# A fused two-layer decoder on one core: the top-32 search cut into fifteen pieces of two segments per head, and GpSimd adding two pairs of heads with one instruction

## The chip, the cores and the metric

The kernel runs as one launch on one core of a Trainium2 chip. The metric is the device time of that launch in microseconds (us), as the median over runs. A core has five engines with instruction streams of their own that meet only at semaphores: TensorE (PE), VectorE (DVE), ScalarE (ACT), GpSimd (POOL) and SyncE (SP).

## The reference, cut to what matters

The whole is a decoder of two layers over `x` (1024 tokens x 128 numbers) and a context of 6404 rows x 96. The stage that the change touches is the sparse cross-attention of the second layer:

```python
B, T, DT, G, DV = ...            # here 1, 1024, 128, 6404, 96
H, DH, K_TOP = 4, 32, 32
Q = (x_text @ Wq).reshape(Bb, Tt, H, DH)
K = (x_vision @ Wk).reshape(Bb, Gg, H, DH)
scores = jnp.einsum('bthd,bghd->bhtg', Q, K) / np.sqrt(DH)
topv, topi = jax.lax.top_k(scores, K_TOP)
probs = jax.nn.softmax(topv, axis=-1)
attn = zeros_like(scores).at[bi, hi, ti, topi].set(probs)
attn_mean = attn.mean(axis=1)                       # over the four heads
c_t = jnp.einsum('btg,bgd->btd', attn_mean, x_vision @ Wv)
```

For each token and head the 32 largest of 6404 scores are wanted, their softmax, and the mean of the four heads' sparse weights multiplied with the context.

## The kernel before, in words

`weigh_program` (called by `search_and_weigh`) does this stage. Tokens go in 8 tiles of 128, each with 4 heads, so 32 heads in all. Two streams of work run side by side.

**Search.** For each head, PE computes the scores piece by piece into one of 3 PSUM banks (`SEARCH_BANKS`), by two bf16 matmuls a piece (`score_unit`, L1461 and L1463). There are 13 pieces, twelve of 512 columns and one of 260 (`PIECES`). DVE takes the eight largest of each segment of a piece with `dve.max` (L1665, MAX8 in the profile): a 512 piece has three segments of 170 or 171 columns, the 260 piece two of 130, so a head has 38 segments (`N_SEG`) and 304 candidates in `kept`. Then `pick` takes the 32 largest of these candidates in eight steps, which are woven into the search of the next head: one reduction (L1640), four MAX8 (L1648) and three replacements (L1646), all over the whole row of candidates. If a segment's eighth value is above the 32nd found, the head is flagged and `search_general` and `weigh_again` do the work anew in another way.

**Weighing.** A step `n` is one piece of `PIECES` for one tile, so there are 104 steps. For each of its 4 heads PE computes the scores again into one of 3 other banks, ACT takes the exponential into `e` (L1847; a ring of 4 steps), and values under the 32nd are set to zero: heads 0 and 1, and head 2 in every other step, on DVE (L1695); the rest by a mask that ACT makes (L1825, L1826) and POOL multiplies (L1718). In the last tile DVE does all four, and adds two of them. POOL then adds the four heads to `mean` (L1722, L1726, L1727), PE transposes it (L1739), ACT copies the result (L1804), and PE multiplies with the context (L1752). At the first step of each tile the limits of the four heads are made by a short chain between DVE and ACT (L1678, L1853, L1682, L1856, L1686 to L1688, L1859).

**Order.** Each engine's order is written out: loops over `G` (a step) and `sub` (a head), and in each such slot one piece of the search and one head of the weighing. The weighing of a tile runs `LAG` = 15 steps behind the search, so the search is alone for 15 steps at the start, and the weighing is alone for the last 15.

## Time and profile before

| what | value |
|---|---|
| median of 3 runs | 1744.25 us (1743.5 to 1744.35) |
| profiled execution, its time | 1739.54 us |
| its span, first to last instruction | 1737.8 us |
| mean granted TensorE clock | 0.912 of full |
| the stage's first matmul, last DVE search instruction, last POOL addition (starts) | 642.5 us, 1211.3 us, 1275.25 us |

Times in the rows count from the start of the span. In a row of a timeline the number in square brackets is how long the engine was idle before it, and what released it. "Busy" is the union of the instructions' durations; consecutive instructions on DVE overlap in their durations, so what an instruction costs in a dense row is the distance between starts.

### The profile page before, as it was taken

To read this page: it belongs to the slowest core of one execution; us is meant where nothing else is said; L and a number is where in the kernel's file an instruction comes from. 1 tells how busy PE (TensorE), PEld (TensorE's weight loads), DVE (VectorE), ACT (ScalarE), POOL (GpSimd) and SP (SyncE) were. 2 spreads that over 40 slices of the span, in tenths; PEclk is the share of its full clock that TensorE was granted. 3 is DMA by queue.
4 is the path that set the end of the run, shared out by engine and by line. 5 is a ranking of instruction groups with operands and counts; after the bars stand their busy time and mean duration, and the time that the engine had idled before them with its cause. 6 is when DMAs were issued, how large, how long until landed. Compare 5 with 4: busy or idle time off the path is not lost. (4 is left out here: it accounts for less than half of the span.)

```text
span 1737.8 us, 19863 instructions
## 1 busy us (share of the span) xinstructions
PE 1420.6 (82%) x6581; PEld 752.1 (43%) x6637; DVE 1288.2 (74%) x3067; ACT 930.5 (54%) x1452; POOL 697.0 (40%) x529
## 2 busy tenths in 40 slices
PE   5777899899986747889898888988859339999798
PEld 2233344345544421355454554545547223333365
DVE  4998677855427539999999999999857666777433
ACT  4665212556521310788888888888831225666321
POOL 0664312012000000698898988989930030000012
PEclk9899899999987867999999999999888758999999
DMA  6000110000009320000000000000011030000000
GB/s 145 1 1 0 39 61 29 0 1 0 0 19 198 68 64 1 1 1 1 1 1 1 1 1 1 1 1 1 1 27 71 22 80 1 1 1 1 1 1 12
DMA packets 30968, 37.36 MB, mean 21 GB/s; under 512 B 13889, under 2 KB 24096, under 8 KB 29732
## 3 DMA queue, kind: packets, MB, share of 16 engines
q1 hardware_dynamic: 29312, 24.19, 5.1%
q10 hardware_dynamic: 1544, 11.79, 3.3%
q8 instruction: 56, 0.92, 0.2%
q14 instruction: 56, 0.46, 0.1%
HBM read 29.73 MB, written 6.24 MB: 21 GB/s over the span
## 5 line engine op out<-in xcount | busy, mean ns | idle before, releaser
L1461 PE MATMUL psum<-film_ka,film_context_qa 97*128 97x512 bf16 (+1 forms) x832 | 326.0, 393 | 86.8 <-DVE search_and_weigh_e L1695 36.5
L1665 DVE MAX8 search_and_weigh_kept<-psum 128x8 f32<-128x171 f32 (+2 forms) x1216 | 330.1, 324 | 0.2
L1463 PE MATMUL psum<-film_kb,film_context_qb 128*128 128x512 bf16 (+1 forms) x777 | 302.0, 390 | 0.0
L1847 ACT ACTIVATE search_and_weigh_e<-psum,search_and_weigh_bias 128x512 f32<-128x512 f32 (+1 forms) x416 | 267.5, 665 | 58.0 <-PE psum L1463 54.7
L1695 DVE SCALAR_TENSOR_TENSOR search_and_weigh_e<-psum,film_context_top,search_and_weigh_e 128x512 f32<-128x512 f32 (+1 forms) x283 | 200.0, 714 | 15.5 <-ACT search_and_weigh_e L1847 14.0
L1718 POOL TENSOR_TENSOR search_and_weigh_e<-search_and_weigh_e,search_and_weigh_keep 128x512 f32<-128x512 f32 (+1 forms) x133 | 150.6, 1132 | 108.6 <-ACT search_and_weigh_keep L1826 105.3
L1461 PEld LDWEIGHTS psum<-film_ka,film_context_qa 97*128 97x128 bf16 x832 | 86.3, 104 | 229.8 <-DVE search_and_weigh_e L1695 95.5
L1722 POOL TENSOR_TENSOR search_and_weigh_mean<-search_and_weigh_e 128x512 f32<-128x512 f32 (+1 forms) x104 | 133.4, 1283 | 11.5 <-DVE search_and_weigh_e L1695 4.4
L1752 PEld LDWEIGHTS psum<-ctx_rows,search_and_weigh_mean_T 128*128 128x128 f32 (+1 forms) x816 | 124.1, 195 | 31.3 <-issue 5.2
L2959 POOL TENSOR_TENSOR residual<-residual,top_expert_kept 128x1024 f32<-128x1024 f32 x7 | 16.5, 2355 | 292.2 <-DVE top_expert_kept L2916 292.2
L1727 POOL TENSOR_TENSOR search_and_weigh_mean<-search_and_weigh_mean,search_and_weigh_e 128x512 f32<-128x512 f32 (+1 forms) x104 | 127.9, 1230 | 8.2
L2722 DVE TENSOR_REDUCE gqa_attend_low<-psum 128x1 f32<-128x128 f32 (+7 forms) x128 | 94.0, 754 | 43.2 <-PE psum L2641 40.7
L1752 PE MATMUL psum<-ctx_rows,search_and_weigh_mean_T 128*128 128x96 f32 (+1 forms) x816 | 121.0, 271 | 1.0
L1726 POOL TENSOR_TENSOR search_and_weigh_e<-search_and_weigh_e 128x512 f32<-128x512 f32 (+1 forms) x91 | 111.8, 1229 | 7.1
L2759 ACT ACTIVATE gqa_attend_prob<-psum 128x512 f32<-128x512 f32 x192 | 84.9, 486 | 49.6 <-PE psum L2654 48.9
L1039 ACT ACTIVATE cross_attention_prob<-psum 128x1024 f32<-128x1024 f32 (+1 forms) x51 | 51.8, 1019 | 97.1 <-PE psum L998 96.4
L340 POOL TENSOR_TENSOR mamba_drive<-mamba_relu,mamba_b_all 128x1024 f32<-128x1024 f32 x32 | 77.2, 2414 | 64.7 <-ACT mamba_b_all L465 33.6
L985 PE MATMUL psum<-cross_attention_prob,ctx_rows 128*97 128x512 f32 (+1 forms) x204 | 98.2, 604 | 4.6 <-ACT cross_attention_prob L1039 4.6
L1825 ACT ACTIVATE search_and_weigh_keep<-search_and_weigh_e,search_and_weigh_below 128x512 bf16<-128x512 f32 (+1 forms) x133 | 93.5, 703 | 12.7 <-POOL search_and_weigh_mean L1727 12.2
L998 PE MATMUL psum<-oss_attention_qc_shifted,ctx_T 97*128 97x512 f32 (+1 forms) x204 | 99.3, 610 | 0.8 <-ACT oss_attention_qc_shifted L1030 0.8
L1463 PEld LDWEIGHTS psum<-film_kb,film_context_qb 128*128 128x128 bf16 x832 | 84.5, 102 | 33.4 <-issue 6.0
L1739 PE MATMUL psum<-ident,search_and_weigh_mean 128*128 128x128 f32 (+1 forms) x408 | 81.3, 281 | 11.7 <-ACT search_and_weigh_mean_T L1804 9.3
(544 smaller groups left out, 2660.1 us busy)
## 6 DMA issues: line engine op xcount, KB each, us to landing
film_kb<-film_k_rows ACTq DMA_DIRECT2D x4, 1601.0 KB
film_ka<-film_k_rows ACTq DMA_DIRECT2D x3, 1601.0 KB
ctx_T<-in_ctx_T SPq DMA_DIRECT2D x1, 2401.5 KB
gqa_experts_w<-in_L_ffn_W SPq DMA_DIRECT2D x1, 2048.0 KB
film_convolve_back<-in_dft_back SPq DMA_DIRECT2D x1, 1728.0 KB, 11.9
film_k_rows<-cross_attention_film_hi SPq DMA_DIRECT2D x6, 256.0 KB, 2.0
film_k_rows<-cross_attention_film_mid SPq DMA_DIRECT2D x6, 256.0 KB, 2.0
film_k_rows<-cross_attention_film_low SPq DMA_DIRECT2D x6, 256.0 KB, 2.0
```

The lines of the kernel that those rows point to most:

```text
L985: last = pe.matmul(ps[0:CA, 6 + n, :], ctx[0:rows, k, :], prob[0:rows, k % 3, n * HALF:(n + 1) * HALF], start=k == 0, stop=k == KT - 1)
L998: last = pe.matmul(ps[0:rows, 2 * (k % 2) + n, :], ctx_T[:, k * P:k * P + rows], qc_shifted[:, n * HALF:(n + 1) * HALF], start=True, stop= ...
L1461: pe.matmul(out, a["qa"][0:ROWS, h, rows], a["ka"][0:ROWS, h, c + b:c + b + cols], start=True, stop=False)
L1463: last = pe.matmul(out, a["qb"][:, h, rows], a["kb"][:, h, c + b:c + b + cols], start=False, stop=True)
L1665: last = dve.max(kept[:, h % 2, first + s, :], bank[:, lo:hi])
L1695: dve.scalar_tensor_tensor(out=w, in0=weigh_bank(n, h), scalar=a["top"][:, NH * i + h, TOP - 1:TOP], in1=w, op0=ALU.is_ge, op1=ALU.mult).t ...
L1718: link(pool.tensor_tensor(w[h], w[h], keep[:, k % KEEPS, 0:width], ALU.mult))
L1722: link(pool.tensor_tensor(out, w[0], w[1], ALU.add))
L1726: link(pool.tensor_tensor(w[2], w[2], w[3], ALU.add))
L1727: pool.tensor_tensor(out, out, w[2], ALU.add).then_inc(mean_ready, 1)
L1752: last = pe.matmul(ps[:, 7, 0:DC], mean_T[0:r, n % 2, b:b + P], ctx[0:r, (c + b) // P, 0:DC], start=c + b == 0, stop=c + b + r == S2)
L1847: act.activation(e[:, n % RING, sub, 0:PIECES[u][1]], ps[:, SEARCH_BANKS + q % WEIGH_BANKS, 0:PIECES[u][1]], ACT.Exp, bias=bias[:, i % 2, ...
```

## The change

The search no longer uses the weighing's pieces. A head's 6404 columns are cut into 30 nearly equal segments of 213 or 214 columns, two to a piece, so 15 pieces of 426 or 427 columns in place of 13. As there are 13 slots of the weighing per head and 15 pieces, `searched_at` deals them: in slots 6 and 12 of each 13, two pieces stand, in the others one. On POOL, two adds of two heads each (`w[0]+w[1]` to `mean`, `w[2]+w[3]` in place) become one in-place instruction over both pairs, and the last add takes `w[0]+w[2]`. In the last tile POOL's adds stay as they were. The core of the diff:

```diff
-def segments(width):
-    n = -(-width // 171)
-    edges = [round(k * width / n) for k in range(n + 1)]
-    return list(zip(edges[:-1], edges[1:]))
-N_SEG = sum(len(segments(w)) for _, w in PIECES)
+SEARCHES, PER_PIECE = 15, 2
+N_SEG = SEARCHES * PER_PIECE
+SEARCH_EDGES = [round(k * S2 / N_SEG) for k in range(N_SEG + 1)]
+
+def search_columns(u):
+    edges = SEARCH_EDGES[PER_PIECE * u:PER_PIECE * (u + 1) + 1]
+    return edges[0], edges[-1] - edges[0], [(lo - edges[0], hi - edges[0]) for lo, hi in zip(edges[:-1], edges[1:])]
...
+    def searched_at(G, sub):
+        k = NH * G + sub
+        return range(k * SEARCHES // NCH, (k + 1) * SEARCHES // NCH)
...
         for G in range(STEPS + LAG + 1):
             for sub in range(NH):
-                r = NH * G + sub
-                head, after = r // NCH - 1, r % NCH
+                for r in searched_at(G, sub):
+                    head, after = r // SEARCHES - 1, r % SEARCHES
...
             pool.wait_ge(w_ready, masks_done(n + 1))
-            if n >= MEANS:
-                pool.wait_ge(mT_psum, n - MEANS + 1)
-            link(pool.tensor_tensor(out, w[0], w[1], ALU.add))
             if last_tile(n):
+                if n >= MEANS:
+                    pool.wait_ge(mT_psum, n - MEANS + 1)
+                link(pool.tensor_tensor(out, w[0], w[1], ALU.add))
                 pool.wait_ge(summed_ready, n + 1 - (NT - 1) * NCH)
+                pool.tensor_tensor(out, out, w[2], ALU.add).then_inc(mean_ready, 1)
             else:
-                link(pool.tensor_tensor(w[2], w[2], w[3], ALU.add))
-            pool.tensor_tensor(out, out, w[2], ALU.add).then_inc(mean_ready, 1)
+                pairs = e[:, n % RING, :, 0:width].rearrange("p (a b) k -> p a b k", b=2)
+                link(pool.tensor_tensor(pairs[:, :, 0, :], pairs[:, :, 0, :], pairs[:, :, 1, :], ALU.add))
+                if n >= MEANS:
+                    pool.wait_ge(mT_psum, n - MEANS + 1)
+                pool.tensor_tensor(out, w[0], w[2], ALU.add).then_inc(mean_ready, 1)
...
-                search(NH * G + sub + SEARCH_LEAD)
+                for r in searched_at(G, sub):
+                    search(r + SEARCH_LEAD)
```

On POOL, the first two steps of the weighing read before:

```order
L1718 TENSOR_TENSOR search_and_weigh_e<-search_and_weigh_e,search_and_weigh_keep 128x512
L1722 TENSOR_TENSOR search_and_weigh_mean<-search_and_weigh_e 128x512
L1726 TENSOR_TENSOR search_and_weigh_e<-search_and_weigh_e 128x512
L1727 TENSOR_TENSOR search_and_weigh_mean<-search_and_weigh_mean,search_and_weigh_e 128x512
L1718 TENSOR_TENSOR search_and_weigh_e<-search_and_weigh_e,search_and_weigh_keep 128x512 x2
```

The same place after the change (L1725 is the former L1718, L1735 the new add of two pairs, L1738 the last add):

```order
L1725 TENSOR_TENSOR search_and_weigh_e<-search_and_weigh_e,search_and_weigh_keep 128x512
L1735 TENSOR_TENSOR search_and_weigh_e<-search_and_weigh_e 128x2x512
L1738 TENSOR_TENSOR search_and_weigh_mean<-search_and_weigh_e 128x512
L1725 TENSOR_TENSOR search_and_weigh_e<-search_and_weigh_e,search_and_weigh_keep 128x512 x2
L1735 TENSOR_TENSOR search_and_weigh_e<-search_and_weigh_e 128x2x512
```

Three additions a step have become two, and the first stands where an instruction of half its width stood.

On DVE, just behind the limits of a tile (the small operations on `bias` and `least`), before:

```order
L1688 TENSOR_TENSOR search_and_weigh_least<-film_context_top,search_and_weigh_bias 128x4
L1695 SCALAR_TENSOR_TENSOR search_and_weigh_e<-psum,film_context_top,search_and_weigh_e 128x260
L1665 MAX search_and_weigh_kept<-psum 128x8 x6
L1695 SCALAR_TENSOR_TENSOR search_and_weigh_e<-psum,film_context_top,search_and_weigh_e 128x512
L1665 MAX search_and_weigh_kept<-psum 128x8 x3
L1695 SCALAR_TENSOR_TENSOR search_and_weigh_e<-psum,film_context_top,search_and_weigh_e 128x512
L1665 MAX search_and_weigh_kept<-psum 128x8 x3
L1695 SCALAR_TENSOR_TENSOR search_and_weigh_e<-psum,film_context_top,search_and_weigh_e 128x512
L1665 MAX search_and_weigh_kept<-psum 128x8 x3
L1640 TENSOR_REDUCE film_context_eighth<-search_and_weigh_kept 128x1
```

After the change (L1695, L1702, L1672 and L1648 are the former L1688, L1695, L1665 and L1640):

```order
L1695 TENSOR_TENSOR search_and_weigh_least<-film_context_top,search_and_weigh_bias 128x4
L1702 SCALAR_TENSOR_TENSOR search_and_weigh_e<-psum,film_context_top,search_and_weigh_e 128x260
L1672 MAX search_and_weigh_kept<-psum 128x8 x4
L1702 SCALAR_TENSOR_TENSOR search_and_weigh_e<-psum,film_context_top,search_and_weigh_e 128x512
L1672 MAX search_and_weigh_kept<-psum 128x8 x2
L1702 SCALAR_TENSOR_TENSOR search_and_weigh_e<-psum,film_context_top,search_and_weigh_e 128x512
L1672 MAX search_and_weigh_kept<-psum 128x8 x2
L1702 SCALAR_TENSOR_TENSOR search_and_weigh_e<-psum,film_context_top,search_and_weigh_e 128x512
L1672 MAX search_and_weigh_kept<-psum 128x8 x5
L1648 TENSOR_REDUCE film_context_eighth<-search_and_weigh_kept 128x1
```

A slot has two segments where it had three, and the doubled slot at the end of a head has four, with a fifth that begins the next head.

On PE, at a doubled slot after the change (L1464 and L1466 are the former L1461 and L1463; 426 or 427 columns are a piece of the search, 512 one of the weighing; L1763 and L1750 the former L1752 and L1739):

```order
L1466 MATMUL psum<-film_kb,film_context_qb 128x512
L1750 MATMUL psum<-ident,search_and_weigh_mean 128x128 x2
L1464 MATMUL psum<-film_ka,film_context_qa 128x426
L1466 MATMUL psum<-film_kb,film_context_qb 128x426
L1464 MATMUL psum<-film_ka,film_context_qa 128x427
L1466 MATMUL psum<-film_kb,film_context_qb 128x427
L1464 MATMUL psum<-film_ka,film_context_qa 128x512
```

Before, one pair of L1461 and L1463 for the search stood there, ahead of the pair for the weighing; now the weighing's matmul stands behind two pairs.

## Rows read from the trace of the kernel before

**Rows 1.** Busy time of each engine over the span, from the page.

```profile
PE 1420.6 (82%) x6581; PEld 752.1 (43%) x6637; DVE 1288.2 (74%) x3067; ACT 930.5 (54%) x1452; POOL 697.0 (40%) x529
```

**Rows 2.** Windows of the stage; columns: PE, PEld, DVE, ACT, POOL busy, PEclk, DMA.

```profile
646.60:703.90 57.30, 42.86 (x120) 10.95 (x123) 57.06 (x232) 3.65 (x6) 0.00 (x0) 0.74 0.00 1
...
784.87:859.93 75.06, 66.57 (x357) 37.72 (x363) 72.71 (x235) 64.33 (x113) 68.91 (x58) 0.98 0.00 1
...
935.01:1010.10 75.09, 66.62 (x357) 37.80 (x363) 72.78 (x235) 64.41 (x113) 68.87 (x59) 0.98 0.00 1
...
1233.00:1276.00 43.00, 38.19 (x243) 27.62 (x247) 40.43 (x61) 36.31 (x62) 37.60 (x27) 1.00 0.01 1
```

**Rows 3.** Timeline of POOL: first weighing, two full steps, a tile's boundary.

```profile
709.82 1.16 POOL L1718 TENSOR_TENSOR search_and_weigh_e<-search_and_weigh_e,search_and_weigh_keep 128x512 f32<-128x512 f32 x1 [89.38 <-ACT search_and_weigh_keep L1826]
...
922.85 2.38 POOL L1718 TENSOR_TENSOR search_and_weigh_e<-search_and_weigh_e,search_and_weigh_keep 128x512 f32<-128x512 f32 x2
925.31 1.26 POOL L1722 TENSOR_TENSOR search_and_weigh_mean<-search_and_weigh_e 128x512 f32<-128x512 f32 x1
926.66 1.27 POOL L1726 TENSOR_TENSOR search_and_weigh_e<-search_and_weigh_e 128x512 f32<-128x512 f32 x1
928.01 1.26 POOL L1727 TENSOR_TENSOR search_and_weigh_mean<-search_and_weigh_mean,search_and_weigh_e 128x512 f32<-128x512 f32 x1
...
929.98 0.73 POOL L1722 TENSOR_TENSOR search_and_weigh_mean<-search_and_weigh_e 128x260 f32<-128x260 f32 x1
...
935.01 1.16 POOL L1718 TENSOR_TENSOR search_and_weigh_e<-search_and_weigh_e,search_and_weigh_keep 128x512 f32<-128x512 f32 x1 [2.67 <-ACT search_and_weigh_keep L1826]
...
1233.00 1.29 POOL L1722 TENSOR_TENSOR search_and_weigh_mean<-search_and_weigh_e 128x512 f32<-128x512 f32 x1
```

**Rows 4.** Waits in one period, 935.01 to 1010.1: waiter, releaser, total us, times, longest.

```profile
PEld psum L1461 <- DVE search_and_weigh_e L1695: 12.3, 19, 1.9
ACT search_and_weigh_e L1847 <- PE psum L1463: 7.0, 9, 1.4
POOL search_and_weigh_e L1718 <- ACT search_and_weigh_keep L1826: 5.4, 2, 2.7
...
ACT search_and_weigh_keep L1825 <- POOL search_and_weigh_mean L1727: 1.7, 3, 1.1
DVE search_and_weigh_e L1695 <- ACT search_and_weigh_e L1847: 1.6, 4, 0.6
```

**Rows 5.** Timeline of DVE where the search is alone.

```profile
656.55 0.20 DVE L1640 TENSOR_REDUCE film_context_eighth<-search_and_weigh_kept 128x1 f32<-128x38 f32 x1
...
662.17 2.98 DVE L1665 MAX8 search_and_weigh_kept<-psum 128x8 f32<-128x171 f32 x12
...
693.21 0.20 DVE L1640 TENSOR_REDUCE film_context_eighth<-search_and_weigh_kept 128x1 f32<-128x38 f32 x1
```

**Rows 6.** Durations by tile `kept`: min/median/max ns, first and last start, forms.

```profile
L1665 DVE MAX8 search_and_weigh_kept<-psum x1216: 273/325/345, 646.6 to 1211.3; 128x8 f32<-128x171 f32 x110, 128x8 f32<-128x170 f32 x55, 128x8 f32<-128x130 f32 x9
L1648 DVE MAX8 film_context_top<-search_and_weigh_kept x128: 450/457/478, 657.2 to 1216.7; 128x8 f32<-128x304 f32 x128
```

**Rows 7.** Groups of POOL over the whole span: count, busy us, mean ns, idle.

```profile
L340 POOL TENSOR_TENSOR mamba_drive<-mamba_relu,mamba_b_all 128x1024 f32<-128x1024 f32 x32 | 77.2, 2414 | 64.7 <-ACT mamba_b_all L465 33.6 <-DVE mamba_relu L280 28.6 <-issue 2.1
L646 POOL TENSOR_TENSOR ss_attention_s4d_i_decay<-cross_attention_s4d_ar,ross_attention_s4d_index 128x1024 f32<-128x1024 f32 x16 | 31.2, 1960 | 131.1 <-DVE ss_attention_s4d_i_angle L612 127.5 <-DVE ross_attention_s4d_turns L544 3.6
L2959 POOL TENSOR_TENSOR residual<-residual,top_expert_kept 128x1024 f32<-128x1024 f32 x7 | 16.5, 2355 | 292.2 <-DVE top_expert_kept L2916 292.2
```

**Rows 8.** Timeline of DVE: the limits of the first tile, and of a later one.

```profile
702.13 0.15 DVE L1686 TENSOR_TENSOR search_and_weigh_bias<-search_and_weigh_total,film_context_top 128x4 f32<-128x4 f32 x1
...
924.26 1.00 DVE L1686 TENSOR_TENSOR search_and_weigh_bias<-search_and_weigh_total,film_context_top 128x4 f32<-128x4 f32 x1 [0.66 <-ACT search_and_weigh_total L1856]
925.49 1.10 DVE L1688 TENSOR_TENSOR search_and_weigh_least<-film_context_top,search_and_weigh_bias 128x4 f32<-128x4 f32 x1
```

**Rows 9.** Timeline of PE at full clock, weighing and search of one slot.

```profile
907.07 0.38 PE L1461 MATMUL psum<-film_ka,film_context_qa 97*128 97x512 bf16 x1
907.29 0.38 PE L1463 MATMUL psum<-film_kb,film_context_qb 128*128 128x512 bf16 x1
...
907.73 0.28 PE L1461 MATMUL psum<-film_ka,film_context_qa 97*128 97x260 bf16 x1
907.84 0.28 PE L1463 MATMUL psum<-film_kb,film_context_qb 128*128 128x260 bf16 x1
```

More of the change, by code:

```diff
@@ L1619, in search_piece @@
     def search_piece(r):
-        if not searching or r >= STEPS * NH:
+        if not searching or r >= NT * NH * SEARCHES:
             return None
-        i, s = divmod(r, NH * NCH)
-        return i, s // NCH, s % NCH
+        i, s = divmod(r, NH * SEARCHES)
+        return i, s // SEARCHES, s % SEARCHES
+    def searched_at(G, sub):
+        k = NH * G + sub
+        return range(k * SEARCHES // NCH, (k + 1) * SEARCHES // NCH)
     def limits_tile(G):
@@ L1638, in pick @@
             if step == 0:
-                dve.wait_ge(searched, NCH * (j + 1))
+                dve.wait_ge(searched, SEARCHES * (j + 1))
                 dve.reduce_max(eighth[:, j:j + 1], kept[:, k, :, 7], AX).then_inc(picked, 1)
@@ L1653, in vector @@
             for sub in range(NH):
[L1654 to L1672 removed]
+                for r in searched_at(G, sub):
+                    head, after = r // SEARCHES - 1, r % SEARCHES
+                    picking = searching and 0 <= head < NT * NH and after < PICKS // 2
+                    if search_piece(r):
+                        i, h, u = search_piece(r)
+                        dve.wait_ge(search_done, r + 1)
+                        if u == 0 and i * NH + h >= 2:
+                            dve.wait_ge(picked, PICKS * (i * NH + h - 1))
+                        bank = ps[:, r % SEARCH_BANKS, :]
+                        for s, (lo, hi) in enumerate(search_columns(u)[2]):
+                            last = dve.max(kept[:, h % 2, PER_PIECE * u + s, :], bank[:, lo:hi])
+                            if s == 0 and picking:
+                                pick(head, 2 * after)
+                        last.then_inc(searched, 1)
+                    elif picking:
+                        pick(head, 2 * after)
+                    if picking:
+                        pick(head, 2 * after + 1)
                 i = limits_tile(G)
```

19 lines of the change are left out of this document (1 added, 18 removed).

## The prediction

> **What bounds the kernel now.** I read the page's busy line first: PE has the largest share of the span, DVE the next, POOL only 40% [rows 1]. These are averages over stages that share nothing with this one, so I went to the windows. The stage has three stretches. From 646.6 to 703.9 the search is alone and DVE is busy 57.06 of 57.30 us. In the middle the picture repeats with a period of 75.08 us per tile. From 1233 to 1276 the last tile is weighed alone [rows 2]. The change touches the first two.
>
> In a middle period DVE is busy 72.75 us, POOL 68.9, PE 66.6, ACT 64.4 [rows 2]. POOL looks as if it had 6 us to spare, but its timeline says otherwise. An instruction starts about 0.08 us after the one before has ended (925.31 + 1.26 to 926.66, and to 928.01) except before a mask, and there is one real gap per tile, 2.67 us at the first step of a tile (935.01) [rows 3]. So 75.08 - 2.67 = 72.4 us per tile is POOL work with its fixed gaps. POOL is a chain without a break but one from 709.82 to 1233.0, that is 523.2 us for seven tiles: 7 x 72.4 plus six gaps of 2.7 [rows 3]. DVE, at 72.75 of 75.08, is as full. The waits say that the two hold each other: PE waits for DVE to free a bank (12.3 us a period), ACT for PE (7.0), POOL for ACT's mask (5.4, in 2 waits), ACT for POOL in turn (1.7), and DVE for ACT only 1.6 [rows 4]. Two engines are the bound together; making one faster would give little, and the change makes both faster.
>
> **DVE's part.** Twelve segments in a dense row take 2.98 us; less the last one's own 0.325 [rows 6] that is 2.655/11 = 0.241 us from start to start, with change of piece 0.245 [rows 5]. How much of it goes with the columns? Between MAX8 of 130 and of 171 columns in PSUM the durations differ by 325 - 273 = 52 ns, 1.27 ns a column; from 171 (PSUM) to 304 (SBUF) by 132 ns, 0.99 a column [rows 6]. I take 1.04, nearer to the wider difference, since durations are rounded and 133 columns are the longer lever. The fixed part is then 0.245 - 171 x 0.00104 = 0.067 us (0.028 to 0.076 by the two ends). All 6404 columns are still read, and 38 segments become 30: 8 x 0.067 = 0.54 us per head (0.22 to 0.61). The picking runs over 240 values instead of 304: seven instructions (four L1648, three L1646) x 64 x 1.04 ns = 0.47 us (0.44 to 0.57). Together 1.0 us per head (0.7 to 1.2), 4.0 per tile. Its floor per tile falls from 72.75 to 68.7.
>
> The Trainium skill (Perfetto Trace Analysis, Optimizing Scalar/DVE Operations) gives about 125 ns as DVE's fixed cost per instruction on PSUM. No row here shows that much: the whole start-to-start distance for 171 columns is 0.245 us. By that figure, called an estimate, the eight segments would give 1.0 us instead of 0.54.
>
> **The first stretch.** DVE alone sets it. Two reductions that open a head, 656.55 and 693.21, are three heads apart: 12.22 us per head [rows 5]. The stretch holds 15 steps x 4 slots / 13 = 4.6 heads, before and after, because the dealing keeps 13 slots per head. It shrinks by 4.6 x 1.0 = **4.7 us** (3 to 5.5). PE could spoil this where its clock is at the lower level (0.74 on average here [rows 2]): one piece is then two matmuls of 427 columns. A 512 matmul's start-to-start distance is 0.22 us at full clock [rows 9], so a piece needs 2 x 0.18 = 0.36 us at full and 0.71 at half clock, against DVE's 2 x 0.289 = 0.58. Before, it was 0.86 against 0.74, the same relation, and DVE did not stand still then; three banks and the picking carry it. I cost it at nothing, and its end at 1.7 us off the 4.7.
>
> **POOL's part.** L1722 and L1726, 1.27 us each with 0.08 behind each, are 2.70 us of start-to-start time [rows 3]. The new instruction has 1024 outputs. The nearest rows of that size are 2.355 us (L2959, an in-place add) and 2.414 (L340); L646 with 1.960 is the low end, and 2.62, no gain but one gap, the high end [rows 7]. The slope of POOL's own adds agrees: (1.27 - 0.73)/252 columns = 2.14 ns, so 1.27 + 512 x 0.00214 = 2.37 [rows 3]. I take 2.36 + 0.08 = 2.44: a step saves 0.26 us (0 to 0.66), and the 260 step as much, since it too loses one fixed part. 13 steps: **3.4 us per tile**; POOL's floor falls from 72.4 to 69.0. The mean's wait for PE (`mT_psum`) moves behind the pair add, where it can only come out earlier.
>
> So both floors fall almost equally, to 69.0 and 68.7. The period should follow with its gap of 2.7 on top. Seven tiles of POOL's chain: 7 x 3.4 = 23.8 us, before a debit.
>
> **The debit at the boundary.** DVE's operation L1686 on 4 numbers takes 0.15 us at 702.13, when POOL has not begun, and 1.00 at 924.26: it ends at 925.26, as POOL's masks end (922.85 + 2.38 = 925.23). The next, L1688, takes 1.10 and ends at 926.59, with POOL's L1722 (925.31 + 1.26 = 926.57) [rows 3, 8]. So here a DVE operation on two SBUF operands waits until POOL's running one is over. What POOL then runs is now, in one phase of three, the 2.36 us pair add instead of 1.27. ACT's first exponential of the tile needs L1688, and POOL the masks that follow. The price lies between 0 and 2.5 us a tile (L1688 +1.1, L1686 +1.4). I take 0.8: one time in three 1.1 for L1688, and as often 1.4 for L1686. Seven tiles: -5.6 us.
>
> The Trainium skill (SBUF — State Buffer, Who interferes with whom) says that a DVE instruction with two SBUF inputs contends with a GpSimd one that reads SBUF, and that the loser is blocked for the whole instruction. By that rule, the trace agrees with its 1.00 and 1.10, and a longer POOL instruction is a longer block. It speaks against joining the adds.
>
> **What costs nothing.** PE has 64 more pieces, but the same columns: the distance is 0.22 us for 512 and 0.11 for 260 columns, so it goes with the columns [rows 9]; its 66.6 busy us of 75.1 cover the rest. The last tile is not edited: 43 us, as before [rows 2]. Heads flagged for the general path: worked out on the reference's inputs, none of the 4096 rows and heads has eight of its top values in one segment, with 38 segments or with 30, so `weigh_again` stays empty. If one had, a second pass of some 500 us would follow.
>
> **Sum.** 23.8 - 5.6 + 4.7 = 22.9 us off. The profiled execution took 1739.54 us, so it would be 1716.6; the median of the runs shown stands 4.7 higher, at 1744.25, and I forecast 1744.25 - 22.9 = **1721.3 us**.
>
> **The rivals.**
>
> *Another engine holds the period.* At a period of 72.5 us ACT's 64.4 are 89% and PE's 66.6 are 92% [rows 2], in loops of three banks. ACT already waits for PE and PE for DVE [rows 4]. If half of POOL's gain is lost so, 7 x 1.5 + 4.7 = 15 off: 1729. For it: the table loads and the limits at a boundary do not get shorter. Against: DVE's waits for ACT are small.
>
> *The gap closes too.* DVE's floor was 0.35 us above POOL's, now it is 0.3 below. If the producers thus refill the ring sooner and half of the 2.67 us gap goes, with no block: 7 x (3.4 + 1.3) + 4.7 = 38 off: 1707.
>
> *Doubled slots stall the weighing: slower.* In two slots of 13, PE has two searches before the weighing's matmul, and the second may not start until DVE is done with the slot before. A slot is 75.08/52 = 1.44 us, and the delay up to one piece, 0.58 us. Eight doubled slots per tile, 56 in all: if all is exposed, 56 x 0.58 = 32 us against 23 gained, 1753. It decides from 0.41 us exposed per doubled slot. Against: DVE's doubled slot is itself 0.58 longer, so what PE delivers late is also wanted late, and three banks hold 4 us of weighing.
>
> *The pair add is no cheaper.* If 1024 elements in two strided rows cost twice 1.27 plus 0.08, POOL keeps its 72.4, which with the gap is the old period: only 4.7 off, 1739.5, about the bound of what can be told (0.2%, 3.5 us, is what I take as the measurement's limit). For it: no row has this pattern. Against: all three rows of 1024 are under it.
>
> **How the numbers follow.** The forecast, 1714 to 1727, has 0.58; another engine (to 1734) 0.18; the closed gap 0.11; no cheaper 0.08; the stall 0.05. The range runs from 1709 to 1733: it leaves out most of the closed gap, the last two and the tail of the second. Slower is the stall, 0.04; within 0.2%, 0.05, from the last rival and a stall half exposed; faster 0.91.
>
> **What the changed profile would show.** L1672 at a start-to-start distance near 0.29 us, the heads of the first stretch 11.2 us apart, POOL's first mask near 705. L1735 at 2.36 us (wrong if above 2.6). A period of 72 to 72.6 us, POOL still unbroken but for one gap per tile, of 2.7 to 3.5 us. L1693 and L1695 (the former L1686 and L1688) at 1.0 to 2.4 us. I am wrong if POOL shows gaps within a tile: then the period is set by the loop of DVE, PE and ACT, and the first or the third rival holds.

## The result, and the profile after

The changed kernel takes 1739.44 us (median of 16 runs, 1734.11 to 1742.68), the kernel before 1742.88 (16 runs on the same chips): a ratio of 0.9975 [0.9966, 0.9985]. The ratios leave out three slow runs: 1931.34 us here and 3492.31 in the experiments, both of the kernel before, and 2908.77 of `free_search`. The medians are 3.4 us apart where 22.9 were forecast, and the time is outside the range; the ratio puts the gain at 2.6 to 5.9 us. The profiled execution took 1738.25 us with a span of 1736.5.

First the page: the busy time of each engine, and the groups of the edited instructions.

```profile
PE 1415.3 (82%) x6711; PEld 771.9 (44%) x6765; DVE 1267.0 (73%) x2811; ACT 929.4 (54%) x1452; POOL 680.9 (39%) x438
...
L1672 DVE MAX8 search_and_weigh_kept<-psum 128x8 f32<-128x213 f32 (+1 forms) x960 | 316.7, 375 | 3.8 <-PE psum L1466 3.2
...
L1735 POOL TENSOR_TENSOR search_and_weigh_e<-search_and_weigh_e 128x1024 f32<-128x1024 f32 (+1 forms) x91 | 207.0, 2274 | 7.1
...
L1725 POOL TENSOR_TENSOR search_and_weigh_e<-search_and_weigh_e,search_and_weigh_keep 128x512 f32<-128x512 f32 (+1 forms) x133 | 150.5, 1132 | 124.9 <-ACT search_and_weigh_keep L1838 121.6
```

Both engines did lose work: DVE 21.2 us, POOL 16.1, against [rows 1]. Now the windows (columns as in [rows 2]): the search alone, one period, and the last tile.

```profile
646.60:699.10 52.50, 41.40 (x139) 12.36 (x141) 52.02 (x189) 3.28 (x5) 0.00 (x0) 0.80 0.00 0
...
931.22:1006.39 75.17, 65.37 (x372) 40.38 (x378) 70.39 (x203) 64.21 (x113) 66.57 (x45) 0.98 0.00 1
...
1225.83:1269.74 43.91, 38.78 (x248) 27.98 (x251) 41.39 (x62) 36.96 (x63) 38.10 (x27) 1.00 0.00 1
```

The first exponential starts at 699.11 us instead of 703.54, so the first stretch is 4.4 us shorter. But the period is 75.17 us where it was 75.08, with DVE busy 2.4 us less and POOL 2.3 us less in it. The waits of that period show where POOL's went.

```profile
PEld psum L1464 <- DVE search_and_weigh_e L1702: 8.3, 8, 2.9
...
POOL search_and_weigh_e L1725 <- ACT search_and_weigh_keep L1838: 6.1, 2, 4.3
ACT search_and_weigh_e L1859 <- PE psum L1466: 6.0, 9, 1.0
PE psum L1464 <- DVE search_and_weigh_e L1702: 4.9, 7, 2.5
...
DVE search_and_weigh_e L1702 <- ACT search_and_weigh_e L1859: 3.1, 5, 1.1
...
ACT search_and_weigh_least L1871 <- DVE search_and_weigh_least L1695: 1.2, 1, 1.2
```

POOL waits for a mask 6.1 us in all, in two waits, both at the tile's boundary. Its timeline, from the first mask and over one boundary, is to be read beside [rows 3]:

```profile
705.74 1.16 POOL L1725 TENSOR_TENSOR search_and_weigh_e<-search_and_weigh_e,search_and_weigh_keep 128x512 f32<-128x512 f32 x1 [85.11 <-ACT search_and_weigh_keep L1838]
...
991.30 2.39 POOL L1725 TENSOR_TENSOR search_and_weigh_e<-search_and_weigh_e,search_and_weigh_keep 128x512 f32<-128x512 f32 x2
993.77 2.35 POOL L1735 TENSOR_TENSOR search_and_weigh_e<-search_and_weigh_e 128x1024 f32<-128x1024 f32 x1
996.20 1.26 POOL L1738 TENSOR_TENSOR search_and_weigh_mean<-search_and_weigh_e 128x512 f32<-128x512 f32 x1
999.22 0.68 POOL L1725 TENSOR_TENSOR search_and_weigh_e<-search_and_weigh_e,search_and_weigh_keep 128x260 f32<-128x260 f32 x1 [1.76 <-ACT search_and_weigh_keep L1838]
...
1006.40 1.16 POOL L1725 TENSOR_TENSOR search_and_weigh_e<-search_and_weigh_e,search_and_weigh_keep 128x512 f32<-128x512 f32 x1 [4.33 <-ACT search_and_weigh_keep L1838]
```

The pair add costs what was forecast, 2.35 us. The one gap of 2.67 us per tile became two, 1.76 + 4.33 = 6.09: POOL's whole 3.4 us turned into waiting. Why the masks are late stands in the timeline of DVE, ACT and PE at the same boundary.

```profile
994.05 2.09 DVE L1693 TENSOR_TENSOR search_and_weigh_bias<-search_and_weigh_total,film_context_top 128x4 f32<-128x4 f32 x1 [0.61 <-ACT search_and_weigh_total L1868]
...
996.17 0.17 DVE L1694 TENSOR_SCALAR search_and_weigh_bias<-search_and_weigh_bias 128x4 f32<-128x4 f32 x1
...
996.37 1.10 DVE L1695 TENSOR_TENSOR search_and_weigh_least<-film_context_top,search_and_weigh_bias 128x4 f32<-128x4 f32 x1
...
997.51 0.20 ACT L1871 ACTIVATE search_and_weigh_least<-search_and_weigh_least 128x4 f32<-128x4 f32 x1 [1.22 <-DVE search_and_weigh_least L1695]
...
997.93 0.39 PE L1464 MATMUL psum<-film_ka,film_context_qa 97*128 97x512 bf16 x1 [2.52 <-DVE search_and_weigh_e L1702]
...
999.26 0.63 PE L1464 MATMUL psum<-film_ka,film_context_qa 97*128 97x512 bf16 x1
```

L1693 (before, L1686) on four numbers takes 2.09 us and ends at 996.14, as POOL's pair add does (993.77 + 2.35 = 996.12). L1695 takes 1.10 and ends at 997.47, with POOL's L1738 (996.20 + 1.26 = 997.46). DVE does nothing else for those 3.4 us, so no bank comes free and PE stands still for 2.52 us. Soon after that the granted clock drops; the windows before, in and behind it:

```profile
995.00:998.60 3.60, 1.08 (x8) 0.47 (x6) 3.53 (x7) 2.37 (x5) 2.38 (x2) 1.00 0.00 0
998.70:1001.90 3.20, 3.20 (x12) 1.88 (x11) 3.20 (x9) 2.17 (x4) 2.52 (x3) 0.50 0.00 0
1001.90:1005.00 3.10, 3.10 (x20) 2.00 (x19) 2.56 (x10) 1.53 (x4) 0.17 (x1) 0.97 0.00 0
```

PE was busy 1.08 of 3.60 us, and then runs at 1.2 GHz (PEclk 0.50) just as the new tile's first steps begin: a matmul of 512 columns takes 0.63 us instead of 0.38 [rows 9]. The lower level lasts 3.4 us at each boundary. It did so in the kernel before too, behind two stops of PE of 1.3 to 1.4 us each, so it is not new; the longer standstill is.

How a tile divides, read from the starts of the first exponential of each of its 13 steps (tile 4; the period is the mean of four tiles):

| | last step to step 0 | step 0 to 1 | steps 1 to 12 | period |
|---|---|---|---|---|
| before | 7.62 | 6.02 | 61.49 | 75.07 |
| after | 9.07 | 6.50 | 59.59 | 75.17 |

From step 1 on the change gives 1.9 us. The boundary takes 1.93 back. That is the null result of the middle; the experiments ask whether DVE's wait for POOL is the cause of the second number, and why the first is not 3.4.

### The profile page after: what moved, and what is told of

The parts are those of the page before. It is cut to its first block and busy times, and to the rows that moved or that the text cites. A ratio compares the mean times of both kernels' runs of the same rounds, so it can differ in the third digit from the quotient of the medians.

```text
span 1736.5 us, 19862 instructions
## 1 busy us (share of the span) xinstructions
PE 1415.3 (82%) x6711; PEld 771.9 (44%) x6765; DVE 1267.0 (73%) x2811; ACT 929.4 (54%) x1452; POOL 680.9 (39%) x438
## 3 DMA queue, kind: packets, MB, share of 16 engines
HBM read 29.73 MB, written 6.24 MB: 21 GB/s over the span
## 5 line engine op out<-in xcount | busy, mean ns | idle before, releaser
L1464 PE MATMUL psum<-film_ka,film_context_qa 97*128 97x427 bf16 (+3 forms) x896 | 335.1, 374 | 95.0 <-DVE search_and_weigh_e L1702 41.0
L1672 DVE MAX8 search_and_weigh_kept<-psum 128x8 f32<-128x213 f32 (+1 forms) x960 | 316.7, 375 | 3.8 <-PE psum L1466 3.2
L1466 PE MATMUL psum<-film_kb,film_context_qb 128*128 128x427 bf16 (+2 forms) x843 | 310.9, 370 | 0.0
L1702 DVE SCALAR_TENSOR_TENSOR search_and_weigh_e<-psum,film_context_top,search_and_weigh_e 128x512 f32<-128x512 f32 (+1 forms) x283 | 201.0, 717 | 29.1 <-ACT search_and_weigh_e L1859 25.5
L1735 POOL TENSOR_TENSOR search_and_weigh_e<-search_and_weigh_e 128x1024 f32<-128x1024 f32 (+1 forms) x91 | 207.0, 2274 | 7.1
L1725 POOL TENSOR_TENSOR search_and_weigh_e<-search_and_weigh_e,search_and_weigh_keep 128x512 f32<-128x512 f32 (+1 forms) x133 | 150.5, 1132 | 124.9 <-ACT search_and_weigh_keep L1838 121.6
L1464 PEld LDWEIGHTS psum<-film_ka,film_context_qa 97*128 97x128 bf16 x896 | 92.9, 104 | 213.0 <-DVE search_and_weigh_kept L1672 93.8
L1763 PEld LDWEIGHTS psum<-ctx_rows,search_and_weigh_mean_T 128*128 128x128 f32 (+1 forms) x816 | 125.0, 196 | 32.2 <-issue 6.5
L1763 PE MATMUL psum<-ctx_rows,search_and_weigh_mean_T 128*128 128x96 f32 (+1 forms) x816 | 122.1, 273 | 2.4 <-ACT search_and_weigh_mean_T L1816 0.2
L1738 POOL TENSOR_TENSOR search_and_weigh_mean<-search_and_weigh_e 128x512 f32<-128x512 f32 (+1 forms) x91 | 111.8, 1229 | 7.1
L1466 PEld LDWEIGHTS psum<-film_kb,film_context_qb 128*128 128x128 bf16 x896 | 90.8, 101 | 34.3 <-issue 5.8
L968 PE MATMUL psum<-ctx_T,cross_attention_qc 97*128 97x512 f32 (+1 forms) x208 | 87.3, 576 | 0.7 <-issue 0.7
L924 DVE TENSOR_REDUCE cross_attention_tops<-psum 128x1 f32<-128x1024 f32 (+1 forms) x56 | 61.4, 1109 | 36.1 <-PE psum L968 36.0
```

The costliest lines, as they stand in the source:

```text
L1464: pe.matmul(out, a["qa"][0:ROWS, h, rows], a["ka"][0:ROWS, h, c + b:c + b + cols], start=True, stop=False)
L1466: last = pe.matmul(out, a["qb"][:, h, rows], a["kb"][:, h, c + b:c + b + cols], start=False, stop=True)
L1672: last = dve.max(kept[:, h % 2, PER_PIECE * u + s, :], bank[:, lo:hi])
L1702: dve.scalar_tensor_tensor(out=w, in0=weigh_bank(n, h), scalar=a["top"][:, NH * i + h, TOP - 1:TOP], in1=w, op0=ALU.is_ge, op1=ALU.mult).t ...
L1725: link(pool.tensor_tensor(w[h], w[h], keep[:, k % KEEPS, 0:width], ALU.mult))
L1735: link(pool.tensor_tensor(pairs[:, :, 0, :], pairs[:, :, 0, :], pairs[:, :, 1, :], ALU.add))
```

## The experiments

All eleven kernels were timed in three batches beside the kernel before (its medians there: 1740.69, 1740.40, 1743.27 us), with 4 to 12 runs of each and 17 of the kernel before per batch. Compare kernels of different batches by their ratios. "Starts" are those of the first exponential of a step; they are those of tile 4, while the period is the mean of four tiles. In `search_only`, `pairs_only`, `moved`, `free_all` and `lock_twice`, and in one tile of `free_moved`, tiles differ by 0.8 to 1.6 us, so there the columns need not add up to the period.

| kernel | median us | ratio to before [95%] | period | step 12 to 0, 0 to 1 | steps 1 to 12 |
|---|---|---|---|---|---|
| search_only | 1740.15 | 0.9993 [0.9980, 1.0006] | 75.2 | 7.62, 5.00 | 61.49 |
| pairs_only | 1751.60 | 1.0060 [1.0040, 1.0080] | 75.8 | 9.32, 6.03 | 60.06 |
| free_limits | 1717.66 | 0.9866 [0.9845, 0.9886] | 71.93 | 7.66, 4.60 | 59.68 |
| moved | 1750.54 | 1.0054 [1.0035, 1.0073] | 76.8 | 8.92, 6.24 | 61.10 |
| free_old | 1732.95 | 0.9953 [0.9936, 0.9970] | 73.89 | 8.71, 3.65 | 61.56 |
| free_search | 1730.78 | 0.9930 [0.9914, 0.9946] | 73.51 | 7.37, 4.60 | 61.55 |
| free_pairs | 1729.21 | 0.9933 [0.9919, 0.9948] | 73.42 | 8.28, 3.66 | 61.49 |
| free_all | 1741.14 | 0.9996 [0.9986, 1.0007] | 74.7 | 10.23, 5.07 | 59.59 |
| lock_twice | 1742.31 | 1.0000 [0.9989, 1.0010] | 75.7 | 9.32, 6.31 | 59.62 |
| free_moved | 1723.01 | 0.9889 [0.9865, 0.9914] | 72.68 | 7.61, 3.65 | 61.12 |
| free_keeps4 | 1719.19 | 0.9865 [0.9846, 0.9883] | 71.94 | 7.66, 4.60 | 59.70 |

### One half of the change alone

`search_only` is the changed kernel with POOL's three adds as before; `pairs_only` is the kernel before with the new block of adds.

```diff
 # search_only, against the changed kernel
+            link(pool.tensor_tensor(out, w[0], w[1], ALU.add))
...
-                pairs = e[:, n % RING, :, 0:width].rearrange("p (a b) k -> p a b k", b=2)
-                link(pool.tensor_tensor(pairs[:, :, 0, :], pairs[:, :, 0, :], pairs[:, :, 1, :], ALU.add))
...
-                pool.tensor_tensor(out, w[0], w[2], ALU.add).then_inc(mean_ready, 1)
+                link(pool.tensor_tensor(w[2], w[2], w[3], ALU.add))
+            pool.tensor_tensor(out, out, w[2], ALU.add).then_inc(mean_ready, 1)
```

The "lock" of the expectations is DVE's wait for POOL's running instruction; the "producers" are DVE, PE and ACT, which make what POOL needs.

> The changed kernel with GpSimd's three additions per step as before: only the search is cut anew. Theory A (the boundary): in the changed kernel VectorE's two small additions for a tile's limits wait 2.09 and 1.10 us behind the long pair add, and the producers lose at the boundary what they gain within the tile; with the short additions back, they wait 1.0 and 1.1 again, and the period is GpSimd's 72.4 us plus a smaller gap, about 74.0: some 1732 us. Theory B (GpSimd's chain alone sets the period): 75.1 us a tile as before, only the first stretch shorter: 1739 us. Theory C (the dealing in doubled slots costs the producers some 2 us a tile): 75 to 76 us a tile, 1739 to 1745.

> The kernel before with the pair add alone. Theory A: GpSimd's 3.4 us a tile become a wait, and the longer lock at the boundary costs VectorE 1.1 us a tile: period 75 to 76.2 us, time 1743 to 1751. Theory B: the period follows GpSimd's floor, 71.7 us, 1719 us. Theory C: as the kernel before within 2 us, since it has no doubled slots, unless GpSimd held it: 1741 to 1745.

The search alone gives nothing that can be told (0.9993), not the 1732 us of theory A; the pair add alone makes the kernel slower, by 10.9 us against its batch's median, and its period grows by 0.7 us, as theory A had it, though L1686 grew only by 0.46 us and not by 1.1. Two neighbouring periods of `search_only` show what its mean of 75.2 us hides (PEclk is the third number from the end):

```profile
774.60:848.66 74.06, 64.51 (x370) 39.12 (x377) 69.54 (x203) 64.69 (x114) 68.87 (x59) 1.00 0.00 1
848.66:924.25 75.59, 65.88 (x370) 40.28 (x377) 69.99 (x203) 64.53 (x113) 68.87 (x59) 0.98 0.00 1
```

At two of its six boundaries the clock did not fall, and there the period is 74.1 us, the number of theory A; at the other four it fell for 3.4 us, and the periods behind three of these take 75.4 to 75.6 us (the fourth runs into the last tile). DVE's two waits are the same at all six. So in this kernel the lower clock itself costs 1.3 to 1.5 us a tile, and takes what the new search gives. The limits in `search_only`, and then in `pairs_only`, on DVE:

```profile
921.75 1.02 DVE L1693 TENSOR_TENSOR search_and_weigh_bias<-search_and_weigh_total,film_context_top 128x4 f32<-128x4 f32 x1 [0.61 <-ACT search_and_weigh_total L1864]
```

```profile
928.41 1.46 DVE L1686 TENSOR_TENSOR search_and_weigh_bias<-search_and_weigh_total,film_context_top 128x4 f32<-128x4 f32 x1 [0.66 <-ACT search_and_weigh_total L1860]
```

1.02 where POOL's running instruction is a mask, 1.46 where it is the pair add, 2.09 in the changed kernel, whose operation starts earlier in the pair add. The operation meets the same POOL instruction at each of the six boundaries in both kernels (1.00 to 1.02 us, and 1.46), though their periods vary. Steps 1 to 12 take 61.49 us with the search alone and 60.06 with the pair add alone, against 59.6 with both. The pair add alone thus seems to give 1.4 us there, but behind a boundary that has grown by 1.7, and the two are not independent; the kernels without the wait, below, are the cleaner test of whether two engines hold the period.

### The limits without a second input from SBUF

`free_limits` computes the same eight numbers with operations that read one tensor and take the other number as an operand of one column.

```diff
-link(dve.tensor_tensor(b, total[:], top[:, :, 0], ALU.add))
-link(dve.tensor_scalar(b, b, -1.0, None, ALU.mult))
-dve.tensor_tensor(least[:, i % 2, :], top[:, :, TOP - 1], b, ALU.add).then_inc(bias_ready, 1)
+for k in range(NH):
+    last = dve.tensor_scalar(b[:, k:k + 1], total[:, k:k + 1], top[:, k, 0:1], -1.0, ALU.add, ALU.mult)
+    last.then_inc(chain_dve, 1)
+limits_made[0] += NH
+dve.wait_ge(chain_dve, limits_made[0])
+for k in range(NH):
+    last = dve.tensor_scalar(least[:, i % 2, k:k + 1], top[:, k, TOP - 1:TOP], b[:, k:k + 1], None, ALU.add)
+last.then_inc(bias_ready, 1)
```

> The changed kernel, but a tile's limits (bias, least) are made per head by operations with one tensor operand in SBUF and a per-partition scalar, so that they need not wait for GpSimd. Theory A: these operations take some 0.1 us each instead of 3.2 us for both, the gap of GpSimd at the boundary falls from 6.1 to about 3 us, the period from 75.17 to 72.3: 1719 us. Theory B: no change, 1739. Theory C: a third of it, 1733, since the producers' loop within the tile still holds.

Its timeline at a boundary: POOL's pair add, DVE's eight operations within it, then PE.

```profile
985.41 2.35 POOL L1741 TENSOR_TENSOR search_and_weigh_e<-search_and_weigh_e 128x1024 f32<-128x1024 f32 x1
...
985.69 0.58 DVE L1694 TENSOR_SCALAR search_and_weigh_bias<-search_and_weigh_total,film_context_top 128x1 f32<-128x1 f32 x4 [0.61 <-ACT search_and_weigh_total L1874]
...
986.30 0.58 DVE L1700 TENSOR_SCALAR search_and_weigh_least<-film_context_top,search_and_weigh_bias 128x1 f32<-128x1 f32 x4
...
987.33 0.39 PE L1464 MATMUL psum<-film_ka,film_context_qa 97*128 97x512 bf16 x1 [0.27 <-DVE search_and_weigh_e L1708]
```

Eight operations end in 1.19 us, while POOL's instruction goes on; before the edit, two of the three ran until POOL's ended. PE stands 0.27 us at this place instead of 2.52 (its longest stop near the boundary is now 0.93 us), and at none of the six boundaries does the clock fall. Its period's windows row:

```profile
844.05:915.99 71.94, 64.09 (x373) 39.39 (x378) 67.97 (x208) 64.01 (x115) 66.53 (x46) 1.00 0.00 1
```

3.24 us per tile come back, against 2.9 in theory A; DVE's wait and the lower clock are both gone, and the run does not separate their shares. With `free_keeps4` it is the fastest kernel of the study, 1.34% under the kernel before. The Trainium skill (SBUF — State Buffer, Who interferes with whom) says that a DVE instruction with two SBUF inputs contends with a GpSimd one that reads SBUF, and one with a single SBUF input, outside the modes that use both ports, does not. Both halves show in this pair of timelines.

### The same edit on the other three kernels

The diff above was laid on the kernel before (`free_old`), on `search_only` (`free_search`) and on `pairs_only` (`free_pairs`), which makes a table of all eight combinations.

> The kernel before (38 segments, three short additions) with the limits by operations of one SBUF operand. The lock theory: VectorE's 2.1 us at the boundary become about 1.2 us, and PE's idle time there shrinks; GpSimd's floor of 72.4 us with a gap near 2 us is left, a period near 74.3: some 5 us off, 1735. If GpSimd's chain was the bound before, with its gap of 2.7 untouched: 1741, no change.

> The search cut anew and the limits free of the lock, GpSimd's three short additions kept. If GpSimd's floor of 72.4 us then binds: a period of 73.5 to 74.5 and 1728 to 1735. If the pair add brings nothing even without the lock, it is as fast as the kernel with all three, 1718.

> The pair add and the limits free of the lock, the search as before (38 segments, no doubled slots). VectorE's floor is 72.75 less some 0.9, so 71.8 us, with the 2.35 to 3 us that it idles: a period near 74.3, 1736. If the pair add alone was worth its 3.4 us once the lock is gone: 72, 1720.

Periods in us:

| limits | neither | search | pair add | both |
|---|---|---|---|---|
| as written | 75.07 | 75.2 | 75.8 | 75.17 |
| one input | 73.89 | 73.51 | 73.42 | 71.93 |

With the limits out of POOL's way the halves give 0.4 and 0.5 us and together 2.0: neither engine alone, as the prediction had it, but 2.0 and not 3.4. Steps 1 to 12 say the same: 61.56, 61.55 and 61.49 us, and 59.68 only with both. `free_old` and `free_search` came out near what was expected; `free_pairs` (1729.21 us, 73.42) fell between its two expectations, 1736 and 1720. With the limits as written the same edits give +0.1, +0.7 and +0.1. The wait for POOL cost the kernel before 1.2 us a tile already, and costs the changed one 3.24. The difference, 2.06, is what the change pays at the boundary.

POOL's gaps say where the other 1.4 us are. `free_old` has 1.19 + 0.15 = 1.34 us of them in a tile, and 72.4 + 1.34 = 73.7 is about its period. `free_limits` has 2.41 + 0.49 = 2.90, and 69.0 + 2.9 = 71.9 is its period. POOL's own work fell by 3.4 and its waiting rose by 1.56, since the engines that feed it gained only 1.9 in steps 1 to 12. In a period of `free_limits` none of the waits of DVE, PE and ACT whose end the profile can place (all but 1.7 us of ACT's) was ended by POOL, where ACT had waited 1.7 us for it in the kernel before [rows 4]. That points to their own loop as what sets the period.

### The subtraction rewritten too

`free_all` is `free_limits` with the one remaining two-input operation, on 128 columns, written in the same way.

```diff
-dve.tensor_tensor(shifted[:], top, top[:, :, 0:1].to_broadcast([P, NH, TOP]), ALU.subtract).then_inc(found, 1)
+for k in range(NH):
+    last = dve.tensor_scalar(shifted[:, k, :], top[:, k, :], top[:, k, 0:1], None, ALU.subtract)
+last.then_inc(found, 1)
```

> The changed kernel with all three small additions of a tile's limits (shifted too, now four subtractions of 32 columns with a per-partition scalar) free of the lock. Shifted took 0.48 us against 0.28 unlocked, on ACT's way to the limits (1.2 us of waiting): at most 0.3 us a tile less than with two of them freed, 1716. If the 32-column form contends as well, 1718 to 1720.

This missed: 1741.14 us, all of the gain of `free_limits` lost. The timeline of DVE and ACT, and the group of the new operation with its durations (least, median, most, in ns):

```profile
991.31 2.72 DVE L1686 TENSOR_SCALAR search_and_weigh_shifted<-film_context_top 128x32 f32<-128x32 f32 x4
...
994.07 0.31 ACT L1873 ACTIVATE search_and_weigh_shifted<-search_and_weigh_shifted 128x128 f32<-128x128 f32 x1 [3.40 <-DVE search_and_weigh_shifted L1686]
```

```profile
L1686 DVE TENSOR_SCALAR search_and_weigh_shifted<-film_context_top x28: 227/849/2327, 768.1 to 1216.8; 128x32 f32<-128x32 f32 x28
```

The four took 2.72 us where the single operation had taken 0.48. The group is of 28 operations at seven boundaries, which took from 227 to 2327 ns. POOL at the same place:

```profile
991.63 1.26 POOL L1746 TENSOR_TENSOR search_and_weigh_mean<-search_and_weigh_e 128x512 f32<-128x512 f32 x1
992.85 1.15 POOL L1733 TENSOR_TENSOR search_and_weigh_e<-search_and_weigh_e,search_and_weigh_keep 128x512 f32<-128x512 f32 x1
```

The last of the four ends at 994.03, with POOL's L1733 (994.00); the third, which the merged line does not show by itself, ends at 992.93, with L1746 (992.89). The first two fit in around the change of POOL's instruction. So one input isn't enough: at 32 columns this form waits for POOL as well, and may do so more than once in a row of four, and at one column it doesn't. The Trainium skill (the same section) says that the two-port modes of `tensor_scalar` contend with GpSimd too. That would fit the 32 columns; no run here varies the width between 1 and 32, so where it starts is open.

### A second waiting operation

`lock_twice` is the changed kernel with L1695 issued twice.

```diff
+link(dve.tensor_tensor(least[:, i % 2, :], top[:, :, TOP - 1], b, ALU.add))
 dve.tensor_tensor(least[:, i % 2, :], top[:, :, TOP - 1], b, ALU.add).then_inc(bias_ready, 1)
```

> The changed kernel with the addition that makes `least` done twice in a row, so that VectorE stands behind GpSimd once more at each boundary; unlocked it takes 0.16 us. Theory A (the lock at the boundary sets the period): the extra one waits for the end of another GpSimd instruction, 1.1 to 2.4 us a tile, and PE's clock falls at each boundary: 8 to 20 us longer, 1748 to 1759. If the producers had slack there: 1739 to 1741.

It was meant to add one more block, and did not: DVE's two operations, and POOL's two around them.

```profile
924.18 1.10 DVE L1695 TENSOR_TENSOR search_and_weigh_least<-film_context_top,search_and_weigh_bias 128x4 f32<-128x4 f32 x1
...
925.32 0.16 DVE L1697 TENSOR_TENSOR search_and_weigh_least<-film_context_top,search_and_weigh_bias 128x4 f32<-128x4 f32 x1
```

```profile
924.00 1.26 POOL L1740 TENSOR_TENSOR search_and_weigh_mean<-search_and_weigh_e 128x512 f32<-128x512 f32 x1
...
927.23 0.68 POOL L1727 TENSOR_TENSOR search_and_weigh_e<-search_and_weigh_e,search_and_weigh_keep 128x260 f32<-128x260 f32 x1 [1.96 <-ACT search_and_weigh_keep L1840]
```

The extra operation starts at 925.32, when POOL's add has ended (925.26) and POOL waits for a mask until 927.23. It takes 0.16 us. The miss says the same thing from the other side: an operation with two inputs is slow only while POOL runs one. The period grew by 0.5 us even so, and the ratio from 0.9975 to 1.0000, which is neither of the two expectations; PE's stop is 2.7 us here instead of 2.5, and at one of the six boundaries the clock fell for 6.8 us instead of 3.4.

### The doubled searches moved away from the boundary

`moved` deals the eight doubled slots of a tile to slots 17 to 49 instead of evenly over the 52; `free_moved` is the same with the limits of `free_limits`.

```diff
+DOUBLED = (17, 22, 26, 31, 35, 40, 44, 49)
...
+        def first(k):
+            tile, slot = divmod(k, NH * NCH)
+            return tile * NH * SEARCHES + slot + sum(d < slot for d in DOUBLED)
-        return range(k * SEARCHES // NCH, (k + 1) * SEARCHES // NCH)
+        return range(first(k), first(k + 1))
```

> The changed kernel with the eight doubled slots of a tile moved to slots 17 to 49 of its 52, away from the boundary (slots 0 to 14), where two to three of them stood. Theory A: VectorE has some 1.2 us less to do around the boundary, the period falls by about 1 us: 1732. Theory C (doubled slots hold the producers wherever they stand): no change, 1739. If a doubled slot costs nothing anywhere: 1739 as well, and then search_only tells whether the lock is the cause.

> The changed kernel with limits free of the lock, and the eight doubled slots of a tile moved to slots 17 to 49. With the lock the same move cost 1.6 us a tile, and PE's clock was low for 6.8 us at each boundary instead of 3.4. If the clock was the reason, it stays high now and the place of the doubled slots matters little: period 71.5 to 72.3, 1715 to 1720. If doubled slots away from the boundary are worse by themselves: 73.5, 1729.

Both are slower than their even pair, `moved` by 1.6 us a tile, `free_moved` by 0.75. `moved` was expected to gain 1 us; `free_moved`, at 72.68, lies between its two expectations. With the limits as written, PE's clock was at the lower level 6.8 us per tile instead of 3.4; that PE had fewer searches to do around the boundary is my reading of it. Four tiles of `moved`, and the same window of the changed kernel:

```profile
860.00:1160.00 300.00, 259.21 (x1453) 158.88 (x1478) 275.53 (x792) 251.90 (x440) 263.56 (x177) 0.96 0.00 1
```

```profile
860.00:1160.00 300.00, 260.93 (x1479) 161.45 (x1505) 280.90 (x807) 256.17 (x448) 265.71 (x180) 0.98 0.00 1
```

But `free_moved`, where the clock fell once in the four tiles, is slower too. Its steps 1 to 12 take 61.1 us instead of 59.7, and POOL has gaps away from the boundary, which `free_limits` has not:

```profile
1025.11 1.16 POOL L1736 TENSOR_TENSOR search_and_weigh_e<-search_and_weigh_e,search_and_weigh_keep 128x512 f32<-128x512 f32 x1 [0.69 <-ACT search_and_weigh_keep L1849]
...
1041.76 1.16 POOL L1736 TENSOR_TENSOR search_and_weigh_e<-search_and_weigh_e,search_and_weigh_keep 128x512 f32<-128x512 f32 x1 [0.61 <-ACT search_and_weigh_keep L1849]
```

So doubled slots that stand closer together do hold up the weighing. The rival at its full price, 32 us, is excluded by the even dealing, whose POOL waits at the boundary alone; a small cost of the doubled slots there too is not, since no run has 30 segments without them.

### A fourth buffer for masks

`free_keeps4` is `free_limits` with `KEEPS = 4` in place of 3, to ask whether POOL's remaining 2.9 us are a full ring of masks.

> The changed kernel with limits free of the lock and a ring of 4 masks between ScalarE and GpSimd instead of 3. GpSimd still has gaps of 0.4 to 2.9 us at the boundary, 2.95 us a tile in all. If ScalarE's masks come late because they wait for a place in this ring: period 70.5 to 71.5, 1709 to 1715. If they come late because the exponentials do: no change, 1718.

The period is 71.94 us, as with three, and the time is within the spread (1719.19 against 1717.66). ACT's masks are not late for want of a buffer. That they are late because the exponentials are is what is left; no run tests it by itself.

## Why the prediction was wrong

**Right: DVE's and POOL's own costs.** From `free_old` to `free_limits`, where the limits no longer wait for POOL, DVE's busy time falls by 4.0 us per tile (71.99 to 67.97), as forecast. A dense row of four MAX8 takes 1.23 us, so (1.23 - 0.375)/3 = 0.285 us from start to start, forecast 0.289. The pair add: 2.35 against 2.36. POOL's busy time per tile fell by 2.3 us and 13 gaps of 0.08 with it, 3.3 against 3.4. That two engines hold the period together within a tile was right as well. One reading was off without changing a term: the 5.4 us of POOL's waiting for masks count the gap at both ends of the window, and a tile has one, of 2.67.

**The first stretch: nearly.** The reductions that open a head, on DVE:

```profile
655.61 0.19 DVE L1648 TENSOR_REDUCE film_context_eighth<-search_and_weigh_kept 128x1 f32<-128x30 f32 x1
...
690.39 0.19 DVE L1648 TENSOR_REDUCE film_context_eighth<-search_and_weigh_kept 128x1 f32<-128x30 f32 x1
```

Three heads in 34.78 us are 11.59 per head, 0.63 less than before and not 1.0. For 4.6 heads that is 2.9 us. The missing part is what PE was to spoil and was costed at nothing. At the lower clock level a piece costs PE 0.71 us, as the prediction worked out, but DVE only 0.58, and the three banks did not carry it: DVE then had to wait for each piece.

```profile
661.85 0.57 PE L1466 MATMUL psum<-film_kb,film_context_qb 128*128 128x427 bf16 x1
...
662.56 0.57 PE L1466 MATMUL psum<-film_kb,film_context_qb 128*128 128x427 bf16 x1
```

In the three heads nine of the distances from one MAX8 to the next are 0.41 us instead of 0.29, all of them in the stretches at 1.2 GHz: 0.35 us per head, nearly the whole of the missing 0.37. The first exponential came 4.4 us earlier in the profiled pair, but the nine kernels with the new search have it at 700.65 on average (699.11 to 703.21) and the four with the old one at 704.35 (703.54 to 705.65): 3.7 us (3.8 counted from the stage's first matmul), where I had 4.7 and a low end of 3.

**The step that failed first: "The debit at the boundary", 0.8 us a tile.** The mechanism was named there, its size was not right. Two things were wrong in it. I took a chance of one in three; but the order of the instructions, with the waits between the engines, brought the operation to the same POOL instruction at every boundary of the middle, and L1693 took 2.03 to 2.09 us at the six boundaries of the middle (0.47 at the last, 1217.55, and 0.157 in the first tile, before POOL begins). And I priced only the operation itself. Behind it stood all of DVE's queue, so PE had no bank for 2.52 us, and the tile's first steps ran in the 3.4 us of lower clock that follow. With what follows from it, the block costs 3.24 us a tile in the changed kernel and 1.18 in the one before: a debit of 2.06. At six boundaries that is 6 x 2.06 = 12.4 us where I had 5.6: 6.8 more than forecast.

**The step that failed second: "The period should follow with its gap of 2.7 on top".** Without any block, `free_old` to `free_limits`, the period follows by 1.96 us and not by 3.4: 7 x 1.44 = 10.1 us less than forecast. This is near my first rival, which left 1.5 us a tile of POOL's 3.4. POOL's chain is without a break only as long as the masks come in time; the loop of DVE, PE and ACT that makes them gained 1.9 us in steps 1 to 12. No engine of that loop is full in `free_limits` (DVE 67.97 of 71.94, PE 64.09, ACT 64.01), so which link sets 59.6 us stays open. The one edit that changed it is the place of the doubled slots (61.1), so they may have a share in it.

**The sum again.** 22.9 - 6.8 - 10.1 - 1.0 (the first stretch) = 5.0 us, where the medians show 3.4 and the ratio allows 2.6 to 5.9: the three shortfalls account for the miss within what can be told. The two profiled runs by themselves are only 1.3 us apart, and show places that no term of mine covers. In them the stage ended 6.2 us earlier (1269.74 against 1275.98): POOL's first mask 4.1, the seven tiles 3.1, most of it in the last of them, less 0.9 in the weighing of the last tile. Of that the rest of the program gave 4.9 back:

```profile
1269.74:1736.50 466.76, 358.91 (x2187) 199.59 (x2187) 269.26 (x595) 176.16 (x298) 35.29 (x29) 0.86 0.07 20
```

The same instructions (x2187, x595, x298, x29) took 461.8 us in the kernel before, with 118 us of them at the lower clock; here 130. Over all thirteen kernels, whose code behind the stage is the same, four with 117 to 118 us at the lower level took 462, and nine with 121 to 131 took 464 to 468. What makes the clock fall differently in the same code, no run separates. That the two numbers go together is no shown cause, and it hits `free_limits` as much (466.6).

**The rivals.** The closed gap didn't happen: the gap grew. The dearer pair add is refuted by 2.35. The stall of the doubled slots is refuted at its full price, by a POOL that waits at the boundary alone; packed closer, in `moved` and `free_moved`, they do cost. The rule of the Trainium skill that I set against the change (SBUF — State Buffer, Who interferes with whom) was the right one: the pair add by itself is slower by 0.6% (`pairs_only`), and gives 0.5 us a tile once the limits need not wait (`free_pairs` against `free_old`).

## What to carry to other kernels

Before two instructions of one engine are joined, look for what waits until an instruction of that engine is over, and price the block with everything queued behind it, in the phase in which the order really places it: two instructions of four columns a tile, with what queues behind them, cost some 19 us of 1739 here (ratios 0.9975 and 0.9866, or 6 x 3.24). Where the order of the engines is fixed by their waits, an average over phases is no estimate. And when two engines are full, a saving on both is worth what the slowest loop that feeds them gains, so read the starts of the steps beside the busy times.

## What the runs showed of the hardware that I had not expected

- An operation of DVE on 128x4 numbers with both inputs in SBUF took 0.15 us with POOL idle, and up to 2.10 us with a POOL add running, always ending with it. Four tensor_scalar on 128x1, with their second number as an operand, took 0.58 us together beside the same POOL instruction; one on 128x32 took up to 2.33.
- 2.5 us without a matmul at a boundary were followed by 3.4 us of granted clock at 1.2 GHz, beginning a little later, when PE was busy again: the price falls on the first steps of the next tile, not on the stretch before the fall. Without it a period of `search_only` was 1.3 to 1.5 us shorter. PE's stops before it differ: in the kernel before two of 1.3 to 1.4 us went ahead of a fall at all six boundaries; in `search_only` one of 1.05 and one of 1.44 did at four of six; in `free_old` one of 1.33, and in `free_limits` one of 0.93, at none.
- On POOL, joining two adds of 512 columns into one with two strided rows takes 2.35 us against 2 x 1.27 with 0.08 between: 0.27 us less.
